# A GNN block of four layers on one core: node stages with their centring beside the sums, ScalarE taking part of the normalising, and TensorE's blocks put in order by shape

## The reference

```python
h = maximum(layernorm(x), 0)                       # ahead of each layer
x = x + h + segsum(sigmoid(z @ W_f) * softplus(z @ W_s) * exp(-d**2 / 18), dst)   # z = [h[dst], h[src], edge_attr]
x = x + segsum(relu([h[src], h[dst], e] @ W1 + b1) @ W2 + b2, dst)
x = x + fc(relu(gatv2(relu(gatv2(h)))))            # 5 heads, self loops; fc(g) = g @ Wfc + bfc
x = x + (h + elu(batchnorm(degree-scaled sum of h[src] @ W + b)))
```

## Time and profile before

| | us |
|---|---|
| median of 3 runs | 5698.8 (5698.16 to 5701.34) |
| the profiled execution | 5692.45 |
| its span | 5690.7 |

### The profile page before, as it was taken

The page is one execution under the profiler, slowest core; times in us unless marked ns, Lnnn a source line. Parts: engine busy times, 40 slices in busy tenths (PEclk is TensorE's granted clock), DMA queues, the critical chain, the costliest instruction groups (busy, mean ns, idle before and its releaser), DMA issues. The chain is left out here.

```text
span 5690.7 us, 126079 instructions
## 1 busy us (share of the span) xinstructions
PE 4263.5 (75%) x32065; PEld 3093.0 (54%) x32065; DVE 3250.9 (57%) x7165; ACT 3088.8 (54%) x7416; POOL 3317.9 (58%) x3341
## 2 busy tenths in 40 slices
PE   1089996599952999974997679999299896055573
PEld 1067775477741666643773256666177663055552
DVE  3934446688876332237879832233688788722266
ACT  0279996565655444433872234444178423755547
POOL 0966662377733555535878965554188687677720
PEclk6599997799976999986999989999699898577775
DMA  9476664766657445441334454444133333722224
GB/s 250 91 153 149 149 149 84 157 130 128 128 114 194 116 115 116 115 94 31 84 75 94 95 127 115 115 114 115 37 75 83 78 88 79 153 52 52 53 58 142
DMA packets 1392328, 618.39 MB, mean 109 GB/s; under 512 B 876801, under 2 KB 1351357, under 8 KB 1390426
## 3 DMA queue, kind: packets, MB, share of 16 engines
q1 hardware_dynamic: 1307692, 534.90, 39.9%
q0 software_dynamic: 63360, 65.01, 6.9%
q10 hardware_dynamic: 21140, 17.02, 1.1%
HBM read 379.93 MB, written 236.09 MB: 108 GB/s over the span
## 5 line engine op out<-in xcount | busy, mean ns | idle before, releaser
L920 ACT ACTIVATE hot_e<-iota_n,rel 128x256 f32<-128x256 f32 x1176 | 500.9, 500 | 424.2 <-PE part_e L933 418.2
L1964 DVE COPY zT_l<-zTp_l 128x512 f32<-128x512 f32 x196 | 135.6, 692 | 955.3 <-PE alp_l L1882 691.2
L1939 ACT ACTIVATE leak_l<-tp_l,bcat 128x512 f32<-128x512 f32 x588 | 391.8, 686 | 469.6 <-PE tp_l L1894 445.5
L950 DVE TENSOR_TENSOR acc<-acc,part_e 128x128 f32 x1176 | 336.3, 286 | 472.0 <-PE part_e L933 342.6
L933 PE MATMUL part_e<-z_e,hot_e 128*128 128x128 f32 x1568 | 282.5, 354 | 383.8 <-DVE acc L1661 187.0
L1036 POOL DMA_INDIRECT z_l<-g_d,src_i x392 | 384.0, 979 | 316.4 <-PE zTp_l L1075 220.8
L1036 POOL DMA_INDIRECT z_l<-h_d,src_i x392 | 383.8, 979 | 316.6 <-PE zTp_l L1075 220.9
L1036 POOL DMA_INDIRECT z_e<-h_d,src_i x392 | 384.6, 981 | 207.9 <-PE zTp_e L1075 112.9
L1944 ACT ACTIVATE leak_l<-tp_l,bcat 128x256 f32<-128x256 f32 x784 | 307.1, 474 | 350.2 <-PE tp_l L1901 348.4
L933 PEld LDWEIGHTS part_e<-z_e,hot_e 128*128 128x128 f32 x1568 | 260.2, 259 | 406.1 <-DVE acc L1661 187.3
L1170 POOL DMA_INDIRECT z_e<-h_d,row_of_e x392 | 387.2, 988 | 124.6 <-issue 108.8
(11 more groups left out here) (408 smaller groups left out, 11426.3 us busy)
## 6 DMA issues: line engine op xcount, KB each, us to landing
m_d<-m_m SPq DMA_DIRECT2D x196, 138.0 KB
h_d<-h SPq DMA_DIRECT2D x56, 448.0 KB
relb_e<-rel_d SPq DMA_DIRECT2D x196, 128.0 KB
near_e<-h_d SPq DMA_DIRECT2D x392, 64.0 KB
near_e<-g_d SPq DMA_DIRECT2D x392, 64.0 KB
relb_l<-rel_d SPq DMA_DIRECT2D x196, 128.0 KB
near_l<-h_d SPq DMA_DIRECT2D x392, 64.0 KB
z_l<-rest_d SPq DMA_DIRECT2D x196, 128.0 KB
```

Source lines behind the costliest of these rows:

```text
L920: ins = self.nc.scalar.activation(self.hots[k][:, t, :], self.S["iota_n"][:, :], ACT.Abs, scale=-1.0, bias=self.S["rel"][:, ds(n * BLK + t ...
L950: ins = self.nc.vector.tensor_tensor(x, x, part[:, t % 2, :, 0:x.shape[2]], ALU.add)
L1939: nc.scalar.activation(leak[u % 2][:, q, :], tp[q][:, :], ACT.Relu, bias=bcat[:, 0, q:q + 1], scale=1.0 - SLOPE).then_inc(leak_ready, 1)
```

## The change

In `setup` the tiles `bias3` and `ones3` become 128 rows high with zeros below the third row of `bias3`, and `bfc` is cut in the same way into a new tile `bfc3`. In `node_pass` centring goes to GpSimd in all layers, squares to ScalarE as one operation, sums of squares to VectorE. VectorE's order becomes: mean g, reciprocal g-3, sum of squares g-2, sum of g+1, `h` of g-3. The first `ON_ACT` of the 14 tiles of `h` (8 in pass 0, 4 in pass 2, none in pass 3) are made by ScalarE as ReLU with a scale, counted in a new semaphore `n_ha`; all that waited for `n_h` waits for both. `node_tables` gets the same order with `h` all on VectorE, and three `sq` buffers in place of four. In the gated edges all four transposes and the two of `att` come first, then the 16 passes with `near`. The last layer's bias is one product of `ones3` and `bfc3`.

```diff
         w0 = sb("w0", [P, 2 * C])
         w0s = sb("w0s", [P, 2 * C])
         w0a = sb("w0a", [P, 2 * C])
-        bias3 = sb("bias3", [3, BLK * C], BF16)
-        ones3 = sb("ones3", [3, P], BF16)
+        bias3 = sb("bias3", [P, BLK * C], BF16)
+        bfc3 = sb("bfc3", [P, BLK * C], BF16)
+        ones3 = sb("ones3", [P, P], BF16)
         w1ab = sb("w1ab", [P, 2 * C])
         w1t = sb("w1t", [2, P])
...
                 chain(nc.vector.memset(S["w1t"][:, :], 0.0))
                 chain(nc.vector.memset(S["ones3"][:, :], 1.0))
+                chain(nc.vector.memset(S["bias3"][:, :], 0.0))
+                chain(nc.vector.memset(S["bfc3"][:, :], 0.0))
...
-                chain(nc.vector.tensor_copy(S["bias3"][:, :].rearrange("p (q c) -> p q c", q=2), wide(whole[:, :], 1, 2)))
+                chain(nc.vector.tensor_copy(S["bias3"][0:3, :].rearrange("p (q c) -> p q c", q=2), wide(whole[:, :], 1, 2)))
+
+                for i in range(3):
+                    chain(nc.vector.tensor_copy(cut_b[:, 0:C], S["bfc"][0:3, :]))
+                    chain(nc.vector.tensor_copy(cut[:, i, 0:C], cut_b[:, 0:C]))
+                    chain(nc.vector.tensor_tensor(S["bfc"][0:3, :], S["bfc"][0:3, :], cut[:, i, 0:C], ALU.subtract))
+                chain(nc.vector.tensor_scalar(whole[:, 0:C], cut[:, 0, 0:C], ident[0:3, 0:1], None, ALU.mult))
+                for i in range(1, 3):
+                    chain(nc.vector.scalar_tensor_tensor(out=whole[:, 0:C], in0=cut[:, i, 0:C], scalar=ident[0:3, i:i + 1], in1=whole[:, 0:C],
+                                                         op0=ALU.mult, op1=ALU.add))
+                chain(nc.vector.tensor_copy(S["bfc3"][0:3, :].rearrange("p (q c) -> p q c", q=BLK), wide(whole[:, 0:C], 1, BLK)))
...
     TWO = 2 if layer == 3 else DEEP
-    SUMS_ON_ACT = layer in (1, 2)
+    ON_ACT = {0: 8, 2: 4, 3: 0}[layer]
...
+        def normalised(eng, count):
+            need(eng, n_h, count)
+            if ON_ACT:
+                need(eng, n_ha, count)
+
+        def may_write(eng, g):
+            k = g % DEEP
+            if layer != 3:
+                need(eng, n_out[k], outs * (g // DEEP))
+            if layer in (0, 3):
+                need(eng, n_add, g - DEEP + 1)
+            if layer == 3:
+                need(eng, n_dg, g - DEEP + 1)
...
-                def normalise(g):
+                def invert(g):
                     k = g % DEEP
                     dve.wait_ge(n_std, g + 1)
                     nc.vector.reciprocal(rstd[k][:, :], rstd[k][:, :]).then_inc(n_inv, 1)
-                    if layer != 3:
-                        need(dve, n_out[k], outs * (g // DEEP))
-                    if layer in (0, 3):
-                        need(dve, n_add, g - DEEP + 1)
-                    if layer == 3:
-                        need(dve, n_dg, g - DEEP + 1)
+
+                def normalise(g):
+                    k = g % DEEP
+                    may_write(dve, g)
                     dve.wait_ge(n_inv, g + 1)
-                    nc.vector.scalar_tensor_tensor(out=h[k][:, :, :], in0=xc[k][:, :, :], scalar=0.0, in1=bc(rstd[k]),
+                    nc.vector.scalar_tensor_tensor(out=h[k][:, ON_ACT:, :], in0=xc[k][:, ON_ACT:, :], scalar=0.0, in1=bc(rstd[k])[:, ON_ACT:, :],
                                                    op0=ALU.max, op1=ALU.mult).then_inc(n_h, 1)
 
-                def centre(g):
-                    dve.wait_ge(n_mean, g + 1)
-                    need(dve, n_h, g - DEEP + 1)
-                    nc.vector.tensor_tensor(xc[g % DEEP][:, :, :], acc3[:, tiles(g), :], bc(mean[g % DEEP]), ALU.subtract).then_inc(n_cent, 1)
-
+                add_up(0)
                 for g in range(G + 3):
                     if g < G:
-                        add_up(g)
-                    if 2 <= g < G + 2 and not SUMS_ON_ACT:
+                        take_mean(g)
+                    if g >= 3:
+                        invert(g - 3)
+                    if 2 <= g < G + 2:
                         spread(g - 2)
-                    if g >= 3 and SUMS_ON_ACT:
-                        normalise(g - 3)
-                    if g < G:
-                        take_mean(g)
-                        if SUMS_ON_ACT:
-                            centre(g)
-                    if g >= 3 and not SUMS_ON_ACT:
+                    if g < G - 1:
+                        add_up(g + 1)
+                    if g >= 3:
                         normalise(g - 3)
...
             def _(pool):
                 def centre(g):
                     pool.wait_ge(n_mean, g + 1)
-                    need(pool, n_h, g - DEEP + 1)
+                    normalised(pool, g - DEEP + 1)
                     nc.gpsimd.tensor_tensor(xc[g % DEEP][:, :, :], acc3[:, tiles(g), :], bc(mean[g % DEEP]), ALU.subtract).then_inc(n_cent, 1)
...
                 for g in range(G + 4):
-                    if g < G and not SUMS_ON_ACT:
+                    if g < G:
                         centre(g)
                     if layer in (0, 3) and g >= 4:
...
...
                 def square(g):
                     act.wait_ge(n_cent, g + 1)
                     need(act, n_var, g - DEEP + 1)
-                    if SUMS_ON_ACT:
-                        k = g % DEEP
-                        need(act, n_std, g - DEEP + 1)
-                        for b in range(GRP):
-                            ins = nc.scalar.activation(sq[k][:, b, :], xc[k][:, b, :], ACT.Square, accum_out=var[k][:, b:b + 1])
-                        ins.then_inc(n_var, 1)
-                    else:
-                        nc.scalar.activation(sq[g % DEEP][:, :, :], xc[g % DEEP][:, :, :], ACT.Square).then_inc(n_sq, 1)
+                    nc.scalar.activation(sq[g % DEEP][:, :, :], xc[g % DEEP][:, :, :], ACT.Square).then_inc(n_sq, 1)
 
                 def root(g):
                     act.wait_ge(n_var, g + 1)
-                    need(act, n_h, g - DEEP + 1)
+                    normalised(act, g - DEEP + 1)
                     nc.scalar.activation(rstd[g % DEEP][:, :], var[g % DEEP][:, :], ACT.Sqrt, bias=eps[:, 0:1], scale=1.0 / C).then_inc(n_std, 1)
+
+                def normalise(g):
+                    k = g % DEEP
+                    may_write(act, g)
+                    act.wait_ge(n_inv, g + 1)
+                    for b in range(ON_ACT):
+                        ins = nc.scalar.activation(h[k][:, b, :], xc[k][:, b, :], ACT.Relu, scale=rstd[k][:, b:b + 1])
+                    ins.then_inc(n_ha, 1)
...
                     if 1 <= g < G + 1:
                         root(g - 1)
+                    if ON_ACT and 3 <= g < G + 3:
+                        normalise(g - 3)
                     if layer == 3 and g >= 4:
...
-                        sp.wait_ge(n_h, g + 1)
+                        normalised(sp, g + 1)
                         sp.dma_start(h_rows[g], h[k][:, :, :]).then_inc(n_out[two], 16)
...
-        xc, sq, h = (sb(n, [P, GRP, C]) for n in ("xc", "sq", "h"))
+        xc, sq, h = (sb(n, [P, GRP, C], deep) for n, deep in (("xc", DEEP), ("sq", DEEP - 1), ("h", DEEP)))
...
-                    nc.vector.tensor_reduce(var[g % DEEP][:, :], sq[g % DEEP][:, :, :], AX.X, ALU.add).then_inc(n_var, 1)
-
-                def normalise(g):
+                    nc.vector.tensor_reduce(var[g % DEEP][:, :], sq[g % (DEEP - 1)][:, :, :], AX.X, ALU.add).then_inc(n_var, 1)
+
+                def invert(g):
                     k = g % DEEP
                     dve.wait_ge(n_std, g + 1)
                     nc.vector.reciprocal(rstd[k][:, :], rstd[k][:, :]).then_inc(n_inv, 1)
+
+                def normalise(g):
+                    k = g % DEEP
                     need(dve, n_turn, 2 * (g - DEEP + 1))
                     dve.wait_ge(n_inv, g + 1)
                     nc.vector.scalar_tensor_tensor(out=h[k][:, :, :], in0=xc[k][:, :, :], scalar=0.0, in1=bc(rstd[k]),
                                                    op0=ALU.max, op1=ALU.mult).then_inc(n_h, 1)
 
+                add_up(0)
                 for g in range(G + 3):
                     if g < G:
-                        add_up(g)
+                        take_mean(g)
+                    if g >= 3:
+                        invert(g - 3)
                     if 2 <= g < G + 2:
                         spread(g - 2)
-                    if g < G:
-                        take_mean(g)
+                    if g < G - 1:
+                        add_up(g + 1)
                     if g >= 3:
                         normalise(g - 3)
 
...
                     act.wait_ge(n_cent, g + 1)
-                    need(act, n_var, g - DEEP + 1)
-                    nc.scalar.activation(sq[g % DEEP][:, :, :], xc[g % DEEP][:, :, :], ACT.Square).then_inc(n_sq, 1)
+                    need(act, n_var, g - DEEP + 2)
+                    nc.scalar.activation(sq[g % (DEEP - 1)][:, :, :], xc[g % DEEP][:, :, :], ACT.Square).then_inc(n_sq, 1)
...
-    def turn(self, pe, n, u, i, zTp, gathered):
```

(43 more changed lines are left out.)

## The result

The changed kernel takes 5681.4 us (median of 8 runs, 5676.6 to 5689.2) against 5698.1 us (8 runs, 5693.8 to 5703.4) for the kernel before: a ratio of 0.9972, 95% interval 0.9961 to 0.9983. It is faster by 17 us where 34 were forecast: the time lies within the range, but the forecast of the gain was wrong by half. The profiled execution of the changed kernel took 5680.36 us, its span is 5678.6 us, 12.1 less than the span before. The other 4.6 us of the difference of the medians come from the profiled executions: that of before (5692.45 us) was 5.6 us shorter than the median of its runs, that of the changed kernel 1.0 us.

The account below looks back on a forecast made before the run. Stages between barriers were each taken to have their own bound: TensorE in gated edges and second attention_nodes, VectorE-GpSimd exclusion in node passes. Terms 3.6 + 3 + 24 - 13 + 3 - 18 - 37 = -34.4 gave 5664 us, range 5642 to 5686.

Parts of the forecast that it names:

- Second attention_nodes, -37: Last layer's bias as one bf16 pass relieves TensorE; blocks fall from 2.98 to 2.60 us, bound by VectorE and GpSimd: -37 us.
- The rival at 2.8: Second attention_nodes: TensorE not the bound, or VectorE-GpSimd pair given out in another order; 2.8 us a block, 5684 us, chance 0.11.
- Gated edges, -18: Reordered transposes and padded bias cut TensorE to some 5.65 us a block; ScalarE then bounds at 5.97: -18 us.
- one side remark: Gated edges: if only the reordering helped, TensorE would need 5.85 us a block and still not be the bound.
- node_tables, -13: VectorE's round falls to 3.3 us; two stores a round at 215 GB/s then bound it, about 4.3 instead of 4.64: -13 us.
- Node pass 2, +24: Four tiles on ScalarE tie it to GpSimd's xc in a longer circle, 4.54 us a round instead of 3.55: +24 us.
- rival 1: Node pass 2 falls into the short circle, 3.9 to 4.0 us a round; whole 5650 us, chance 0.15.
- Node pass 0, +3: Eight tiles on ScalarE make it and GpSimd run by turns, 4.86 us a round instead of 4.78: +3 us.
- The rival with 7.3 us a round: Node pass 0: mean waits for xc and add of the same round, ScalarE's work follows; +70, 5734 us, chance 0.06.
- Node pass 3, +3: No tile on ScalarE; VectorE and GpSimd exclude each other, rounds come irregularly, 4.9 us on average: +3 us.
- Setup, +3.6: Cutting bfc takes 13 more VectorE steps, 3.1 us, and two memsets 0.5, nothing hiding them: +3.6 us.
- Rival 4: Node passes 0 and 2: Relu and Sqrt share no ScalarE table, two loads a round; over +110, 5775 us, chance 0.01.

Follow-up runs that it names:

- the circle open: Changed kernel with the second attention_nodes' turned-back block and last layer four blocks behind instead of three, total in four buffers: stage 267.9 us instead of 291.6.

## Why the prediction was wrong, and where it was right

- **Second attention_nodes, -37 forecast, -12.1 measured: the step that failed.** The prediction said that VectorE, which waits 0.36 us a block for TensorE, needs 2.62 at most, and took 2.60 from the first attention_nodes. TensorE's saving at the bias was sized rightly (0.12 us from the bias pass to its follower, 0.11 to 0.17 forecast), and so was the bound of the pair: with the circle open, the blocks are 2.58 to 2.66 us apart. What was not done is to follow the ring of waits once TensorE has room: in the second stage, unlike the first, a wait on GpSimd's total stands in TensorE's queue ahead of the next projection. An engine's idle time is not its own to give back when it waits for an engine that waits in turn for it. The times for it were in the trace of before: `turn_back`, the projection, two products and three additions, 5.6 us over a distance of two blocks, 2.8 a block. By them the term could be -17 at most and not -37; measured, the circle runs at 2.86. The rival at 2.8 (5684 us) came within 3 us of the measured time, but by luck: its mechanism was an unlucky turn for the pair, and with the circle cut the pair needs no 2.8.
- **Gated edges, -18: right in size, one side remark wrong.** ScalarE is the bound at 5.96, TensorE has gaps. That the order alone would also do was wrong (629.0 us): the padding carries the gain. The cost of one change of shape shows in the changed kernel and in the one with the old bias: 0.20 us from the last pass of one shape to the first of the other against 0.11 between equals, so 0.09 each; the pass behind that is late too: the first two passes of the projection behind the 3-row bias take 0.33 us (607.36 to 607.69 in the kernel before), the like two in the changed kernel 0.22 (523.21 to 523.43). The Trainium skill, TensorEngine Tiling (Array Packing), Key Properties, says that a change of mode drains TensorE. These rows agree, and they add that a stationary block of 3 rows makes such a change and a block of bf16 beside fp32 of the same size does not.
- **node_tables, -13: right** (-12.7), for the reason given, as the kernel with one store a round shows.
- **Node pass 2, +24: right mechanism, 5 too many.** The circle runs over ScalarE's Relus, `xc`, `mean`, the sum of squares and the root at 4.38 us; the 0.37 us that `xc` was to wait for VectorE's `h` were not there (`xc` is released by ScalarE, 1709.30), while `xc` itself took 1.80 where 1.53 stood in the sum. After some 16 rounds the stage fell into the short circle of rival 1, 3.99 us; what tipped it over is not shown.
- **Node pass 0, +3: right mechanism, 2 too few** (4.94 against 4.86 a round: the 8 Relus take 2.00 and the hand-over to `xc` 0.17, where 1.95 and 0.05 were counted). The rival with 7.3 us a round did not come.
- **Node pass 3, +3: right** (+2.3), with the irregular rounds (3.15 to 6.57 us between two `h`).
- **Setup, +3.6: near what was measured** (+4.2, in a stage that moves by a few us from one execution to the next).
- **Rival 4, a table load in each round: did not come.** Relu follows Sqrt without a gap (206.42, 206.62) and ScalarE's other idle times are ended by `xc`.

One term of seven carried the error. With it at its measured -12.1 the sum would have been -9.5 us, against -12.1 in the traces.

## What to carry to other kernels

When an engine is full and a change relieves it, do not stop at the next engine's busy time: write down every wait that stands in a queue ahead of other work, follow it round, add up the durations, and divide by the distance in blocks. If that is more than any engine's own work, more distance (one more buffer) is what helps, and it helps only after the relief. The same goes for work handed to an idle engine: a buffer that two engines must both leave before it is refilled ties them together. With four buffers two owners were slower than one (143.2 against 138.0 us in pass 0); with five they were faster there (131.3), while in pass 2 the stores left nothing to gain (110.6 against 108.2).

## What had not been expected of the hardware

A stationary block of 3 rows of bf16 costs TensorE a change of shape on both sides, and padding it with zeros to 128 rows, alone, made the gated edges 15.9 us shorter, 0.16 in each of 98 blocks. The chips differ in their gathers by a fifth (740 against 618 us for the gated edges of the same kernel) and hardly elsewhere, so that a change in a gathering stage that is worth 18 us on one may be worth little on another; by the estimate above it was some 2 us.
